# TensorE's products of the attention slots as two halves of 64 rows, and scores without a ring

## What is computed

```python
def _attention(xq, xkv, wq, wk, wv, wo, bo):
    q = (xq @ wq).reshape(B, S, N_HEADS, D_HEAD)
    k = (xkv @ wk).reshape(B, T, N_HEADS, D_HEAD)
    v = (xkv @ wv).reshape(B, T, N_HEADS, D_HEAD)
    attn = jnp.einsum('bihd,bjhd->bhij', q, k) * D_HEAD ** (-0.5)
    attn = jax.nn.softmax(attn, axis=-1)
    out = jnp.einsum('bhij,bjhd->bihd', attn, v).reshape(B, S, D_ATTN)
    return out @ wo + bo
h = _layernorm(x, ln1_g, ln1_b)
x = _attention(h, h, sa_wq, sa_wk, sa_wv, sa_wo, sa_bo) + x
h = _layernorm(x, ln2_g, ln2_b)
x = _attention(h, ctx, ca_wq, ca_wk, ca_wv, ca_wo, ca_bo) + x
h = _layernorm(x, ln3_g, ln3_b)
p = h @ ff_w1 + ff_b1
a, gate = (p[..., :D_FF], p[..., D_FF:])
out = a * jax.nn.gelu(gate, approximate=False) @ ff_w2 + ff_b2 + x
```

## Time and profile before

| what | us |
|---|---|
| median of 3 executions | 1686.05 (1685.7 to 1687.57) |
| the profiled execution | 1686.2 |
| its span in the profile | 1684.4 |
| TensorE busy | 1675.8 (99%) |
| VectorE, ScalarE, GpSimd busy | 1398.6 (83%), 1248.2 (74%), 1082.8 (64%) |
| slots 3 to 255, in the timeline | 27.48 to 1414.91 |

### The profile page before, as it was taken

One profiled execution on the slowest core, in us unless ns is written; L12 is line 12 of the kernel. 1 busy time (PEld: TensorE's weight loads), 2 busy tenths in 40 slices (PEclk: granted clock), 3 DMA queues, 4 the chain that ended last, 5 costly groups with the idle time before them and its releaser, 6 DMA issues.

```text
span 1684.4 us, 39061 instructions
## 1 busy us (share of the span) xinstructions
PE 1675.8 (99%) x11712; PEld 1559.7 (93%) x11712; DVE 1398.6 (83%) x2964; ACT 1248.2 (74%) x3378; POOL 1082.8 (64%) x1804
## 2 busy tenths in 40 slices
PE   9999999999999999999999999999999999999999
PEld 8999999999999999999999999999999999888888
DVE  8887788888888888888888888888889988666665
ACT  7788788888888888888888888888888887222221
POOL 7776577777766666787777777777777565132111
PEclk9999999999999999999999999999999999999999
DMA  7776677778776667887787878787777785112110
GB/s 221 182 178 161 172 205 196 201 201 212 201 180 161 154 168 201 234 220 184 189 212 193 209 191 208 194 214 177 196 182 177 193 224 163 51 50 76 63 39 26
DMA packets 301137, 288.91 MB, mean 172 GB/s; under 512 B 103424, under 2 KB 252032, under 8 KB 300928
## 3 DMA queue, kind: packets, MB, share of 16 engines
q1 hardware_dynamic: 245696, 270.67, 61.6%
q10 hardware_dynamic: 55232, 15.75, 4.0%
HBM read 82.98 MB, written 37.49 MB: 72 GB/s over the span
## 4 chain that ended last, share of the span: by engine, by line
PE 96%; DVE 2%; ACT 1%; issue 0%; ACTq 0%; DMA 0%; POOL 0%; DVEq 0%; POOLq 0%
PE QKB L564 17%; PE PVB L646 14%; PE PTB L577 13%; PE WOP L628 11%; PE VB L499 9%; PE S L467 7%; PE S L466 7%; PE S L1316 5%; PE PTB L1316 5%; PE QKB L546 3%; PE QKB L1338 3%; PE VB L1338 3%; PE QKB L1281 1%; ACT PT L790 0%; DVE NM L979 0%
## 5 line engine op out<-in xcount | busy, mean ns | idle before, releaser
L790 ACT ACTIVATE PT<-S,NM 128x256 f32<-128x256 f32 x1024 | 472.0, 473 | 133.1 <-DVE NM L979 129.9
L894 DVE TENSOR_TENSOR PL<-PTB,PH 128x512 fp32r<-128x512 f32 x512 | 350.8, 686 | 122.5 <-ACT PH L818 120.9
L1175 POOL TENSOR_TENSOR ON<-ON,RB 128x256 f32<-128x256 f32 x256 | 188.6, 737 | 270.6 <-DVE ON L999 248.7
L979 DVE TENSOR_REDUCE NM<-S 128x2 f32<-128x512 f32 x512 | 327.4, 681 | 0.1
L818 ACT ACTIVATE PH<-PTB 128x1024 fp32r<-128x1024 f32 x256 | 264.0, 1031 | 70.6 <-PE PTB L577 70.0
L577 PE MATMUL PTB<-IDN,PT 128*128 128x128 f32 x2048 | 265.4, 273 | 0.1
L466 PE MATMUL S<-RX 128*128 128x256 f32 x1012 | 253.8, 283 | 0.0
L467 PE MATMUL S<-RX 128*128 128x256 f32 x1012 | 253.7, 283 | 0.0
L564 PE MATMUL QKB<-HT,WQ 128*128 128x512 f32 x936 | 242.3, 394 | 0.3
L628 PEld LDWEIGHTS WOP<-WO,OT 128*128 128x128 f32 x1536 | 217.5, 190 | 19.9
L577 PEld LDWEIGHTS PTB<-IDN,PT 128*128 128x128 f32 x2048 | 229.6, 140 | 0.6 <-issue 0.5
(11 more groups left out here) (162 smaller groups left out, 2923.8 us busy)
## 6 DMA issues: line engine op xcount, KB each, us to landing
RX<-QKS SPq DMA_DIRECT2D x506, 192.0 KB, 2.9
RX<-QKS SPq DMA_DIRECT2D x506, 128.0 KB, 2.8
RB<-denominators SPq DMA_DIRECT2D x512, 64.0 KB, 2.7
out_dram<-XR SPq DMA_DIRECT2D x32, 256.0 KB, 3.5
weights_qk<-SPL SPq DMA_DIRECT2D x32, 256.0 KB, 3.4
WQ<-weights_qk SPq DMA_DIRECT2D x24, 256.0 KB, 3.4
rows<-XN SPq DMA_DIRECT2D x23, 256.0 KB, 2.7
rows<-HF SPq DMA_DIRECT2D x22, 256.0 KB, 2.6
```

Of the source, the lines that this page charges most:

```text
L790: last = e.activation(PT[:, c % 2, j * S:(j + 1) * S], S1[:, i, qt * S:(qt + 1) * S], ACT.Exp, bias=NM[:, j:j + 1], accum_out=DEN[:, c % 2 ...
L894: e.tensor_tensor(PL[:, cols], PTB[:, i, :], PH[:, s % 2, cols].bitcast(F32), ALU.subtract).then_inc(a.dve_pl, 1)
L979: e.tensor_reduce(NM[:, i * TT:(i + 1) * TT], S1[:, i, :].rearrange("p (t s) -> p t s", t=TT), AX.X, ALU.max, negate=True).then_inc(a.dve_ ...
```

## The change

From slot 3 on `pe_attention_slot` calls `pe_packed_slot`. Every product of a slot, the transposes too, is made as two products of 64 rows: one on rows 64 to 127 (`LEADS`), one on rows 0 to 63 (`FOLLOWS`), both adding into the same place of PSUM or, for the transposes, each writing its own 64 columns. Products of 512 columns become products of 256 (`UNIT`). TensorE's order alternates between a product on one half of the rows and a product of another kind, into another bank, on the other half: `r` counts such steps. Six new semaphores (`pe_kl`, `pe_vf`, `pe_vl`, `pe_of`, `pe_hl`, `pe_tf`) make the second half of a product wait for the first. The scores of all slots are the twelve products of 64 rows from QKS; the ring RX, its DMAs and semaphores are gone, and QKS has ten units in place of eight. The other engines' loops are as before.

The first phase of a slot (after the six score steps) pairs the first half of the projection with the first halves of the value tile and the output product. The second phase has on rows 64 to 127: value tile, heads, output product, transposes; and on rows 0 to 63: four transposes, projection, four transposes, heads.

```diff
-K1, Q1, K2 = range(3)
-COPIES = 4
+FOLLOWS, LEADS = OWN
+UNIT = 256
...
     if last_alone(k):
-        return (7, 1, 2, 0, 3, 4, 5, 6)[k - LAST]
+        return (8, 9, 0, 1, 2, 3, 4, 5)[k - LAST]
     if alone(k):
-        return (3, 7)[k % 2]
+        return 4 + k % 4
     n, p = place(k)
     u = n // 2 * PAIRS + p
-    return 3 + u % 5 if n % 2 else u % 3
-
-
-def copied(k):
-
-    return (k - DIRECT) // 2 + 1
+    return 4 + u % 6 if n % 2 else u % 4
+
+
+def holder(k):
+
+    return max((m for m in range(k) if unit(m) == unit(k)), default=None)
...
-        QKS = sb("QKS", [P, 8, 4, S], F32R)
+        QKS = sb("QKS", [P, 10, 4, S], F32R)
...
-        RX = sb("RX", [P, 2, 2, 3, S], F32R)
...
         def pe_scores(e, sl):
             c = sl.c
-            if 0 <= c < DIRECT:
-                e.wait_ge(a.dve_lo, c + 1)
+            if sl.has(c):
+                e.wait_ge(a.dve_lo, made(c))
                 sl.wait(e, a.act_exp, 2 * c)
                 for qt in range(TT):
                     for j, (q, k) in enumerate(((1, 0), (1, 2), (3, 0))):
                                             start=j == 0, stop=j == 2)
                             if qt == TT - 1 and j == 2:
                                 last.then_inc(a.pe_s, 1)
-            elif sl.has(c):
-                e.wait_ge(d_dup[c % 2], 16 * COPIES * ((c - 1) // 2))
-                sl.wait(e, a.act_exp, 2 * c)
-                for i in range(2):
-                    for qt in range(TT):
-                        q = RX[:, c % 2, i, Q1, qt * P:(qt + 1) * P]
-                        o = S1[:, i, qt * S:(qt + 1) * S]
-                        e.matmul(o, q, RX[:, c % 2, i, K1, :], start=True, stop=False)
-                        last = e.matmul(o, q, RX[:, c % 2, i, K2, :], start=False, stop=True)
-                    last.then_inc(a.pe_s, 1)
...
+        def packed_fill_units(c):
+
+            j = c + LEAD
+            if last_alone(j):
+                return 11
+            return 10 if joint(j) and j % 2 == 0 and j // 2 // PAIRS * 2 >= B else 12
...
+        def pe_packed_fill(e, c, rows, n):
+
+            first, last = rows == LEADS and n == 0, rows == FOLLOWS and n == packed_fill_units(c) - 1
+            j, k = c + LEAD, c + (AHEAD if first_alone(c + AHEAD) else LEAD)
...
+                    e.wait_ge(d_wq[p // 2 % 2], 16 * 4 * (p // QUAD + 1))
+                if first:
+                    e.wait_ge(a.dve_lo, nth_joint(j))
+                step, half = divmod(n, 2)
+                cut = lambda h: one(h, half)
+                w, wp, act = list(ph.h_passes(0, g % 2, cut) if kind else ph.kv_passes(2, g % 2, cut))[step]
+                weight = w_pair(w, wp, p)
...
+            if rows == FOLLOWS and n == 0:
+                e.wait_ge(a.pe_kl, c - DIRECT + 1)
+            done = e.matmul(QKB[:, half * S:(half + 1) * S], weight[rows], act[rows], start=first, stop=last,
+                            skip_group_check=True)
+            if rows == LEADS and n == packed_fill_units(c) - 1:
+                done.then_inc(a.pe_kl, 1)
+            if last:
+                done.then_inc(fs.pe_raw if j >= ATT else a.pe_qk, 1)
+
...
+        def packed_value_units(c):
+
+            if c + 1 < FIRST_V:
+                return 6
+            if c <= FIRST_V:
+                return 12
+            if c > ATT - QUAD:
+                return 0
+            turn = (c + 3) % QUAD
+            if place(c + 3 - turn)[0] < B:
+                return 6
+            return 6 if turn % 2 else 4
...
+            w, wp, act = passes[step + n // 2]
+            cols = slice(n % 2 * UNIT, (n % 2 + 1) * UNIT)
+            done = e.matmul(VB[:, cols], act[rows, t * P:(t + 1) * P], w_value(w, wp, p, QUAD)[rows, cols],
+                            start=first and opens, stop=last and closes, skip_group_check=True)
+            if rows == FOLLOWS and n == units - 1:
+                done.then_inc(a.pe_vf, 1)
+            if last and not closes:
+                done.then_inc(a.pe_vl, 1)
+            if last and closes:
+                done.then_inc(a.pe_v, 1)
+        def pe_packed_output(e, s, rows, n):
+
+            p = place(s)[1]
+            t, j = divmod(n, 3)
+            op, wp = ((0, 0), (0, 1), (1, 0))[j]
...
+            if rows == LEADS and n == 0:
+                e.wait_ge(a.pe_of, s + 1)
+            done = e.matmul(WOP[:, t * D:(t + 1) * D], OT[rows, op, t * P:(t + 1) * P], WO[rows, p, wp, :],
+                            start=begins(s) and first, stop=ends(s) and last, skip_group_check=True)
+            if rows == FOLLOWS and n == 5:
+                done.then_inc(a.pe_of, 1)
+            if last:
+                done.then_inc(a.pe_wo, 1)
+
+        def pe_packed_head(e, s, rows, n):
+
+            j, i, kt = n // 4, n // 2 % 2, n % 2
+            first, last = rows == LEADS and n == 0, rows == FOLLOWS and n == 7
+            if first:
+                e.wait_ge(a.pl_v, s - s % 2 + 2)
+                e.wait_ge(a.dve_ad, s)
+                e.wait_ge(a.act_ph, s + 1)
+            if rows == LEADS and j and kt == 0:
+                e.wait_ge(a.dve_pl, 2 * s + i + 1)
+            if rows == FOLLOWS and n == 0:
+                e.wait_ge(a.pe_hl, s - DIRECT + 3)
+            cols = slice((i * TT + kt) * S, (i * TT + kt + 1) * S)
+            part = PL[rows, cols] if j else PH[rows, s % 2, cols]
+            done = e.matmul(PVB[:, i * S:(i + 1) * S], VR[rows, s // 2 % 2, kt, s % 2, i * P:(i + 1) * P], part,
+                            start=first, stop=last, skip_group_check=True)
+            if rows == LEADS and n == 7:
+                done.then_inc(a.pe_hl, 1)
+            if last:
+                done.then_inc(a.pe_pv, 1)
+
+        def pe_packed_turn(e, s, rows, n):
+
+            i, kt, qt = n // 4, n // 2 % 2, n % 2
+            if rows == FOLLOWS and n == 0:
+                e.wait_ge(a.act_exp, 2 * s + 2)
+            if rows == FOLLOWS and n % 4 == 0:
+                e.wait_ge(a.dve_pl, 2 * s + i - 1)
+            if rows == LEADS and n % 4 == 0:
+                e.wait_ge(a.pe_tf, 2 * (s - DIRECT + 1) + i + 1)
+            q0 = (i * TT + qt) * S + kt * P
+            to = kt * S + qt * P + rows.start
+            done = e.transpose(PTB[:, i, to:to + P // 2], PT[rows, s % 2, q0:q0 + P], IDN[rows, rows])
+            if rows == FOLLOWS and n % 4 == 3:
+                done.then_inc(a.pe_tf, 1)
+            if rows == LEADS and n == 7:
+                done.then_inc(a.pe_t, 1)
+
+        def pe_packed_slot(e, c):
+
+            fill, value, output = packed_fill_units(c), packed_value_units(c), 6 if c >= 4 else 0
+            pe_scores(e, Slot(c, ATT))
+            for r in range(max(fill, value + output)):
+                if r < fill:
+                    pe_packed_fill(e, c, LEADS, r)
+                if r < value:
+                    pe_packed_value(e, c, FOLLOWS, r)
+                elif r < value + output:
+                    pe_packed_output(e, c - 4, FOLLOWS, r - value)
+            heads, outputs = value, value + 8
+            turns = max(outputs + output, fill + 8)
+            for r in range(max(turns + 8, fill + 16)):
+                if r < value:
+                    pe_packed_value(e, c, LEADS, r)
+                elif heads <= r < heads + 8:
+                    pe_packed_head(e, c - 2, LEADS, r - heads)
+                elif outputs <= r < outputs + output:
+                    pe_packed_output(e, c - 4, LEADS, r - outputs)
+                elif turns <= r < turns + 8:
+                    pe_packed_turn(e, c - 1, LEADS, r - turns)
+                if r < 4:
+                    pe_packed_turn(e, c - 1, FOLLOWS, r)
+                elif r < 4 + fill:
+                    pe_packed_fill(e, c, FOLLOWS, r - 4)
+                elif r < 8 + fill:
+                    pe_packed_turn(e, c - 1, FOLLOWS, r - fill)
+                elif r < 16 + fill:
+                    pe_packed_head(e, c - 2, FOLLOWS, r - 8 - fill)
+            if joint(c + LEAD) and first_alone(c + AHEAD):
+                pe_project(e, c + AHEAD)
...
-        def copy_ring(e, k):
-
-            r, done, u = k % 2, d_dup[k % 2], unit(k)
-            e.wait_ge(a.dve_lo, made(k))
-            e.wait_ge(a.pe_s, 2 * (k - 1))
-            for i in range(2):
-                e.dma_start(RX[OWN[i], r, i, :, :].bitcast(F32), QKS[OWN[i], u, 0:3, :].bitcast(F32)) \
-                    .then_inc(done, 16)
-                e.dma_start(RX[OTHER[i], r, i, K1:Q1 + 1, :].bitcast(F32), QKS[OWN[i], u, 0:4:3, :].bitcast(F32)) \
-                    .then_inc(done, 16)
-
...
 
             e.wait_ge(a.pe_qk, nth_alone(k) + 1)
-            if k >= LAST:
-                held = max(m for m in range(DIRECT, k) if unit(m) == unit(k))
-                e.wait_ge(d_dup[held % 2], 16 * COPIES * copied(held))
-            elif k > DIRECT + 1:
-                e.wait_ge(d_dup[k % 2], 16 * COPIES * copied(k - 2))
-            elif k > 1:
-                e.wait_ge(a.pe_s, 2 * (k - 1))
```

(39 more changed lines are left out.)

78 lines of the change are left out of this document (74 added, 4 removed).

## The result

The changed kernel takes **2163.12 us** (median of four, 2159.88 to 2171.96) against 1686.39 (four executions too): the ratio is **1.2837, 95% interval 1.2819 to 1.2854**, slower. The prediction was 2166. The profiled execution took 2159.88 us, its span 2158.0. The page, for the earlier trace rows: busy time of each engine, the chain's shares, and the group of the heads' first half (busy, mean ns of one, then idle before it and what ended that).

The account below looks back on a forecast made before the run. A loop from the last transpose over PH, PL, maxima and ON to the heads bounds each slot: 4.64 + 2.59 + 0.12 = 7.35 us; 253 slots plus 8 for late ones, +480 us, give 2166 us, range 2090 to 2550.

Parts of the forecast that it names:

- The new bound, and where it sits: TensorE stalls 1.76 us per slot at the heads' first product, waiting for VectorE's sums ON; slot 7.35 us; chance 0.62.
- First head product to last transpose: On TensorE, 8 heads, 6 outputs and 8 transposes: 21 distances, 0.19 + 20 x 0.12 = 2.59 us a slot.
- The slots at the turn of a sequence: VectorE's layernorm and residual work, behind ON and ahead of the low part, doesn't bind: some 1.6 us of room.
- The clock: a rival with 0.04: TensorE's rests drop its clock to 1.2 GHz, steps up to 0.24: 9.92 us a slot, 2817 us; chance 0.04.
- Steps of 0.12 over a long stream: Each TensorE step of two half products takes 0.12 us throughout the slot, as slot 2's pairs show.
- The rival of 0.19: TensorE's half-product steps take 0.19 us: 8.82 us a slot, +852, 2538 us; chance 0.22 for slower steps.
- the one of unlike products: On TensorE, a transpose and another kind of product don't run at once: +1.3 a slot, 2500 us; within slower steps' 0.22.
- TensorE's own work, "worth almost nothing": TensorE's steps per slot without waits: 5.52 us against 5.56 in self attention, 5.28 against 5.33 in cross attention.
- The scores' -0.24: Scores without the ring: eight products become six steps of 0.12, two steps less, -0.24 us a slot.
- the 0.38 of the mode: Entering and leaving 64-row products costs TensorE 0.38 us a visit, paid only in four late slots and once at the end.
- the ring's 0: The removed DMAs, four a slot on SP's queue, hid behind TensorE, so taking them away gains 0.
- The margin of 0.97 in the kernel before: Before the change, the sums ON ended 0.97 us ahead of the heads that need them, counted as time to spare.

Follow-up runs that it names:

- experiment 1: Changed kernel with one additional VectorE maximum (0.60 us) in every slot from 3 on, between PL and the sums ON: 2370.16 us, 1.4043 against the kernel before.
- experiment 3: Changed kernel with VectorE's order made maximum of head 0, sums ON, second half of PL, maximum of head 1: 1877.30 us, 1.1131 against the kernel before.
- experiment 7: As experiment 6, with the second head's four transposes on rows 0 to 63 put behind 5 to 11 projection steps: 1801.41 us, 1.0677 against the kernel before.
- experiment 5: Kernel before with only the scores of every slot made as twelve 64-row products from QKS, without the ring and its DMAs: 1721.34 us, 1.0208.
- experiment 2: Kernel before with an additional 0.60 us VectorE maximum of the first head's scores in every slot from 3 on: 1750.16 us, 1.0377.
- experiment 6: Changed kernel with heads at the slot's end and the next slot's start, PL in two buffers, values' copy behind PH: 1931.11 us, 1.1457 against the kernel before.
- Experiment 4: Changed kernel with eight more 64-row projection products (0.96 us) ahead of the heads in each slot from 121 on: 2125.55 us, 1.2604 against the kernel before.

## Why the prediction was right, point by point

- **The new bound, and where it sits: right.** TensorE rests before the heads' first product in 251 slots. The row's releaser was to be VectorE's ON; the profile says "issue". By the prediction's own words ("if the releaser is another") that would speak against it; experiments 1 and 3, and the 0.10 us behind ON's end in all 252 slots, settle it for ON. I had foretold some 440 us of it; the row has 380.3, because it counts from the modelled end of the record before, 1.51 a slot. From start to start the rest is 1.92, less the step of 0.12 is 1.80, against 1.76 foretold.
- **PH to the end of ON, 4.31 us foretold** (4.34 from the transposes' end, less 0.03): 4.31 (708.09 - 703.78). VectorE's and ScalarE's durations are those of the earlier trace rows.
- **Last transpose to PH:** from its start 0.43, foretold 0.30 (0.27 for the record and 0.03). 0.13 too low.
- **End of ON to the first head product:** 0.10, foretold 0.15.
- **First head product to last transpose:** 2.23, foretold 2.59. This is the mis-sized term. Heads and outputs came as foretold: 14 distances from 708.19 to 709.93 are 1.74, foretold 0.19 + 13 x 0.12 = 1.75. The eight transposes don't take a step of 0.12 each: they start at 709.93 and end their starts at 710.42, seven distances in 0.49, so 0.07, while the heads on the other half start 0.11 to 0.16 apart. I had let each transpose take the step of the product it stands beside. The two halves of TensorE are not in lockstep.
- **So a slot is 0.43 + 4.31 + 0.10 + 2.23 = 7.07,** not 7.35. Over 253 slots that is 71 us less than foretold.
- **What came on top is 69 us beyond 7.07 a slot,** of which 8 were foretold. The late slots 25 to 28 are 9.30, 9.17, 9.18 and 9.17 long, so 8.5 us (8 foretold, +2.0 each; +2.1 measured). Seventy-eight slots that have a stretch at the lower clock in them or in the slot before, and don't stand at the turn of a sequence, hold 46. Twenty-one at the turn of a sequence hold 15; 13 of these have the lower clock beside them too, so the split between the two is rough. Neither was in the sum: **over the slots 71 us too much and 61 too little stood against each other,** which leaves some 10; the part behind the slots came out some 3 longer than foretold and the median lies 3 above the profiled execution, and so the total agrees to 3 us. The mechanism is shown; the agreement of the total to 0.1% is luck.
- **The slots at the turn of a sequence:** the prediction put VectorE's layernorm and residual work "off the loop, with some 1.6 us of room". VectorE at the start of a slot that begins at 781.18:

```profile
780.85 0.69 DVE L1116 TENSOR_TENSOR XR<-WOP,XR 128x512 f32<-128x512 f32 x1 [2.04 <-PE WOP L751]
781.46 1.25 DVE L1051 TENSOR_SCALAR HF<-XR,MV,RSTD 128x256 f32<-128x256 f32 x2
...
782.97 0.65 DVE L1104 TENSOR_TENSOR QKS<-QKB,QKS 128x512 fp32r<-128x512 f32 x1
783.53 0.68 DVE L1090 TENSOR_TENSOR PL<-PTB,PH 128x512 fp32r<-128x512 f32 x1
```

  The residual can only start when the outputs are done, 2.0 us after VectorE's last work; then layernorm and low part follow, and PL0 starts 2.35 into the slot, not 1.45. The room stood ahead of the work, not behind it. This slot is 7.96 long.
- **The clock: a rival with 0.04, and it came true in part.** The prediction argued against it from waits of 0.83 and 1.5 us in the first 27.5 us. Waits that come once are no measure for 1.9 us in every slot. One stretch came at 74 us, the other 40 from 880 us on, most of them in cross attention (from 928 us), where TensorE has less work in a slot and so rests longer; together they cost some 46 us and not 650.
- **Steps of 0.12 over a long stream: right.** From 704.42 to 705.74 the products of rows 0 to 63 have eleven distances in 1.32 us, with as many on the other rows and two loads for each pair. The rival of 0.19 is out, and so is the one of unlike products: the projection ran paired at this pace with value tile, outputs and heads. Beside transposes nothing slowed either: three outputs start at 709.45, 709.57 and 709.69 with four transposes of the other half between them. The Trainium skill's page "TensorE: Matmul & The Clock Gate", section "Wait — 56ns, not 53.3ns?", has some 62 ns for a MATMUL where it isn't decoded in hardware; by it the step would be 0.124 and this stretch 1.36, and the rows show 1.32. The stretch from 708.19 to 710.42 tells more: 42 products start in its 2.23 us, 54 ns apart in the mean, so that figure doesn't hold here.
- **TensorE's own work, "worth almost nothing": right,** by experiment 7's slots of 5.55 in place of 5.56, and 4.98 for the 42 steps of cross attention (5.04 foretold). The scores' -0.24, the 0.38 of the mode and the ring's 0 are right in their sum, 0.14 a slot, by experiment 5.
- **The margin of 0.97 in the kernel before: wrong** by experiment 2, 0.3 to 0.5 us by the estimate there.
- **A slip that changes nothing:** the exponentials were put 2.56 us into the slot. By the earlier trace rows it is 0.15 + (605.49 - 602.99) = 2.65; the changed kernel has 2.86 (706.25 - 703.39).

## What to carry to other kernels

When a change reorders an engine's stream, look for the instruction that others feed and time the whole round, from what starts the feeders to what this instruction lets start: here a reordering that left TensorE's own work unchanged moved one product from behind 5.3 us of cover into the middle of its own round, and the slot became the round. Sum the round term by term, and check each term afterwards, since a total can agree by errors that cancel. Where an engine's order is freed for one reader, ask which other reader of the same chain comes next: experiments 6 and 7 each removed the wait they aimed at and met another.

## What the runs showed of the hardware that I had not expected

- **TensorE's clock fell although no wait at the heads was longer than 2.4 us.** Windows of the changed kernel, two slots, one with a stretch at the lower level and one without (PE busy first, granted clock behind the five busy times):

```profile
950.20:955.00 4.80, 2.93 (x48) 2.65 (x46) 3.80 (x7) 4.04 (x12) 4.15 (x9) 1.00 0.18 30
955.00:958.40 3.40, 3.38 (x34) 3.40 (x36) 0.04 (x1) 0.61 (x2) 0.73 (x1) 0.51 0.08 24
982.20:987.00 4.80, 2.92 (x48) 2.65 (x45) 3.79 (x7) 4.64 (x13) 3.14 (x7) 1.00 0.15 35
987.00:989.20 2.20, 2.19 (x40) 2.20 (x42) 0.24 (x1) 0.60 (x2) 0.87 (x2) 1.00 0.05 14
```

  The first 4.80 us of both slots are alike, with the same rest in them, and only one of them is followed by half clock (0.51, 1.2 GHz). In all, 41 stretches add up to 140 us, all but one of them behind 870 us. Experiment 4 shows that the rest is a condition; what picks the slot stays open. The price is small for its size: 140 us at half clock cost some 46. I read this from the loop, of which TensorE's steps are 2.23 of 7.07 us and only they get longer; no run tests it.
- **More work can be less time:** 0.96 us of products in each slot of the second half saved 38 us (experiment 4).
- **Half transposes of 64 columns start 0.07 us apart** while products of 256 columns on the other 64 rows start 0.11 to 0.16 apart.
- **A visit to 64-row products costs 0.38 us** within a stream of 128-row ones (experiment 5); within a stream that is all of 64 rows, unlike products pair at the same 0.12.
